# A two-layer row-attention kernel: the first layer's order of work rewritten on every engine, one layer-norm step moved to GpSimd, half the first layer's DVE-copied turns put in a score bank, and an output bias carried into the second layer

## What is computed

```python
x = x + L0(group_norm(x))       # group_norm: 32 groups over all rows, tokens and the group's channels
x = x + L1(group_norm(x))

def L0(x):                      # per row m, 8 heads of 32 channels
    x = layer_norm(x) * norm_w + norm_b                 # over channels
    q, k, v = x @ qkv_w
    weights = softmax(q k + x2d @ x2d_w / sqrt(32))     # 256 x 256 per head, full
    gate = sigmoid(x @ gate_w + gate_b)
    return (weights v * gate) @ final_w + final_b

def L1(x):                      # per row, 4 heads of 64 channels
    q, k, v = x @ w_in + b_in
    weights = softmax(where(|i - j| <= 16, q k / 8, -inf))
    return (weights v) @ w_out + b_out
```

## Time and profile before

| | before |
|---|---|
| median of 3 runs | 3757.91 us (3751.88 to 3758.32) |
| the profiled execution, time | 3752.59 us |
| its span, first to last instruction | 3750.7 us |
| PE busy | 3471.7 us, 93% |
| PEld busy | 3013.3 us, 80% |
| DVE busy | 3122.2 us, 83% |
| ACT busy | 2606.5 us, 69% |
| POOL busy | 1992.7 us, 53% |
| granted TensorE clock, mean | 0.977 |

### The profile page before, as it was taken

How to read it: one execution, slowest core, us unless ns; L and a number is a source line. 1 busy time by engine, 2 the same in 40 slices (tenths; PEclk the granted TensorE clock), 3 DMA queues, 4 the chain that set the end, 5 groups by cost and what they waited for, 6 DMA issues and landing times.

```text
span 3750.7 us, 121088 instructions
## 1 busy us (share of the span) xinstructions
PE 3471.7 (93%) x36234; PEld 3013.3 (80%) x36234; DVE 3122.2 (83%) x11357; ACT 2606.5 (69%) x8615; POOL 1992.7 (53%) x3722
## 2 busy tenths in 40 slices
PE   4469999999999999999999999799999999999998
PEld 1157787787878877787787877699999999999998
DVE  4479999999999999999999999677777777777776
ACT  1158888888888888888888888466666666666665
POOL 0046666676766667666666666333333333333333
PEclk8579999999999999999999999899999999999999
DMA  9911111111111111111111111011111111111111
GB/s 364 359 59 48 50 42 50 42 50 48 44 50 42 50 45 48 50 42 50 42 50 48 44 50 43 29 51 50 50 50 50 50 50 50 50 50 50 50 50 46
DMA packets 189031, 238.40 MB, mean 64 GB/s; under 512 B 11824, under 2 KB 176176, under 8 KB 184752
## 3 DMA queue, kind: packets, MB, share of 16 engines
q1 hardware_dynamic: 184368, 204.17, 17.2%
q10 hardware_dynamic: 4608, 33.56, 2.3%
HBM read 170.57 MB, written 67.11 MB: 63 GB/s over the span
## 4 chain that ended last, share of the span: by engine, by line
PE 50%; DVE 16%; issue 12%; POOL 11%; ACT 5%; DMA 4%; DVEq 1%; ACTq 0%; POOLq 0%; SPq 0%
PE work L458 20%; PE turn L607 7%; POOL prob L354 6%; PE score L590 5%; PE work L467 5%; PE turn L498 5%; PE mix L620 4%; ACT prob L693 4%; PE score L485 3%; DMA x_chunk<-xT 3%; POOL g_tok L368 2%; POOL g_tok L365 2%; DVE kT L936 2%; DVE att L921 2%; DVE y_sb L872 2%
## 5 line engine op out<-in xcount | busy, mean ns | idle before, releaser
L354 POOL TENSOR_SCALAR prob<-prob,row_inv 128x256 f32<-128x256 f32 x2048 | 1049.0, 530 | 682.1 <-DVE row_inv L890 669.6
L458 PE MATMUL work<-src,w 128*128 128x256 f32 x7680 | 1067.5, 288 | 36.9 <-DVE y_sb L872 29.8
L693 ACT ACTIVATE prob<-prob,row_min 128x256 f32<-128x256 f32 x2048 | 1022.8, 504 | 38.9 <-DVE row_min L884 38.8
L458 PEld LDWEIGHTS work<-src,w 128*128 128x128 f32 x7680 | 946.2, 189 | 119.4 <-DVE y_sb L872 59.7
L884 DVE CUSTOM_DVE_ANT_0 prob<-score,neg_bias 128x256 f32<-128x256 f32 x2048 | 753.0, 419 | 111.7 <-PE score L485 100.6
L396 POOL TENSOR_SCALAR prob<-prob,row_inv 128x160 f32<-128x160 f32 x1024 | 387.9, 397 | 814.2 <-DVE row_inv L995 814.2
L756 ACT ACTIVATE prob<-prob,row_min 128x160 f32<-128x160 f32 x1024 | 430.5, 424 | 436.1 <-DVE row_min L988 435.0
L498 PE MATMUL turn<-ident,prob 128*128 128x128 f32 x4096 | 627.3, 276 | 35.3 <-DVE probT L895 29.7
L699 ACT COPY probT<-turn 128x512 f32<-128x512 f32 x512 | 299.4, 585 | 349.8 <-PE turn L498 349.8
L498 PEld LDWEIGHTS turn<-ident,prob 128*128 128x128 f32 x4096 | 463.2, 141 | 78.6 <-POOL prob L354 46.8
L458 PE MATMUL work<-att,wf 128*128 128x256 f32 x3072 | 429.1, 289 | 3.6 <-DVE att L921 2.2
(11 more groups left out here) (86 smaller groups left out, 5021.7 us busy)
## 6 DMA issues: line engine op xcount, KB each, us to landing
pair_chunk<-pairT ACTq DMA_DIRECT2D x32, 1024.0 KB, 7.6
x_chunk<-xT SPq DMA_DIRECT2D x32, 1024.0 KB, 8.0
x_sb<-xT SPq DMA_DIRECT2D x128, 256.0 KB, 3.4
x_tok<-x_nat SPq DMA_DIRECT2D x128, 256.0 KB, 3.4
x1T<-y_sb SPq DMA_DIRECT2D x128, 256.0 KB, 2.2
x_sb<-x1T SPq DMA_DIRECT2D x128, 256.0 KB, 2.9
outT<-y_sb SPq DMA_DIRECT2D x128, 256.0 KB, 2.2
prob<-w_d SPq DMA_DIRECT2D x1, 1024.0 KB, 8.2
```

Source lines behind the costliest of these rows:

```text
L354: pool.tensor_scalar(prob[:, h, ib], prob[:, h, ib], row_inv[:, h, ib:ib + 1], 1.0, ALU.mult, ALU.mult).then_inc(norm_done[0], 1)
L458: ins = pe.matmul(out[:, cb], w[:, of_w, kb, cols + cb * P:cols + (cb + 1) * P], x[:, of_x, kb], start=n == 0, stop=n == len(terms) - 1)
L693: act.activation(prob[:, h, ib], prob[:, h, ib], ACT.Exp, bias=row_min[:, h, ib:ib + 1], scale=-1.0, accum_out=row_sum[:, h, ib:ib + 1]).t ...
```

## The change

All of it but the last item is in the first layer's loop.

- TensorE's order becomes: q(nxt), scores(m, 1), mixes(last, 0), mixes(last, 1), turns(0), t2(far), turns(1), k(nxt), turns(2), turns(3), v(nxt), scores(nxt, 0), turns(4), gate(nxt), turns(5), y(last), turns(6), turns(7). The mixes of a row are thus both done in the turn of the loop after its own.
- turns(3) and turns(7) write the first score bank instead of `turn`. `scores` therefore also waits for DVE's copies of them: scores(m, 1) for the copy of turns(7) of the row before, scores(nxt, 0) for that of turns(3). In return turns(1) and turns(5) directly follow, apart from t2 or the gate, ACT's copy of the turn before them, for which they wait.
- `xn` is computed by GpSimd in place of DVE, in two instructions of 128x256. GpSimd's two steps on `g_tok` work one row further ahead (`ahead`, m+3) and stand apart: the multiplication after norms(m, 1), the addition after norms(m, 2). DVE's layer-norm statistics are for m+3 too, and stand near the end of a turn.
- DVE adds the residual for row m-2 at the start of a turn, as one 128x512 tensor_tensor without a bias in place of two 128x256 instructions with one. The statistics of y are taken every second row, two instructions of 128x512 over two rows, in place of two of 128x256 each row; they stand before the layer-norm statistics, and DVE's last instruction of a turn is the copy of turns(7).
- k uses the same half of `work` as q and the gate; t2, v and y use the other. ACT's order follows.
- The first layer's output bias isn't added to y. The statistics, the second norm's shift and the second layer's output bias (`y_bias`) take it in.

The diff, cut to the order on TensorE, GpSimd and DVE. ACT's reordering, SP's loop and the bias are left out:

```diff
-        gstat1 = sb("gstat1", [P, CB, ROWS, 6])
+        gstat1 = sb("gstat1", [P, CB, ROWS // 2, 6])
...
                 if far.exists:
                     wait(pool, ln_var_done, far.times(1, 1))
                     apart(pool, pool_passed)
                     pool.tensor_tensor(ln_rstd[:], ln_var[:], minus_half[:], ALU.pow).then_inc(ln_rstd_done, 1)
+                    wait(pool, ln_rstd_done, far.times(1, 1))
+                    wait(pool, t2_done, far.times(1, 0))
+                    apart(pool, pool_passed)
+                    for tb in range(TB):
+                        pool.tensor_scalar(xn[:, tb], g_tok[:, far.base % 2, tb], ln_mv[:, tb, 0:1],
+                                           ln_rstd[:, tb:tb + 1], ALU.subtract, ALU.mult).then_inc(xn_done, 1)
+                if m.exists:
+                    norms(m, 1)
+                if ahead.exists:
+
+                    wait(pool, x_tok_in[ahead.base % 2], ahead.times(16, 16, of=2))
+                    wait(pool, xn_done, nxt.times(TB, TB))
+                    apart(pool, pool_passed)
+                    pool.tensor_tensor(g, x_tok[:, ahead.base % 2], gn_row[:, 0].unsqueeze(1).broadcast_to([P, TB, CH]),
+                                       ALU.mult).then_inc(gn_scaled, 1)
+                if m.exists:
+                    norms(m, 2)
+                if ahead.exists:
+                    wait(pool, gn_scaled, ahead.times(1, 1))
+                    pool.tensor_tensor(g, g, gn_row[:, 1].unsqueeze(1).broadcast_to([P, TB, CH]), ALU.add
+                                       ).then_inc(g_done[0], 1)
                 if m.exists:
                     norms(m, 3)
                 if nxt.exists:
                     norms(nxt, 0)
 
-            over_rows(pool, 2, 0, body0)
+            over_rows(pool, 3, 0, body0)
...
+                    wait(pe, turn_done[0][1], r.times(PAIRS0, 2 * hg - 2))
...
                 def turns(h):
                     wait(pe, norm_done[0], m.times(TB * H0, TB * (h + 1)))
-
-                    if h % 2 == 0:
+                    to = turn[:]
+                    if h % HPG == HPG - 1:
+
+                        to = score[:, 0].rearrange("p b t -> p (b t)")
+                        if h < HPG:
+                            wait(pe, min_done[0], m.times(TB * H0, TB * (HPG + 1)))
+                        elif nxt.exists:
+                            wait(pe, min_done[0], nxt.times(TB * H0, TB))
+                    elif h % HPG == 0:
+                        wait(pe, turn_done[0][0], m.times(PAIRS0, h // 2))
+                    elif h % HPG == 1:
+                        wait(pe, turn_done[0][0], m.times(PAIRS0, h // 2 + 1))
+                    else:
                         wait(pe, turn_done[0][1], m.times(PAIRS0, h // 2))
-                    else:
-                        wait(pe, turn_done[0][0], m.times(PAIRS0, h // 2 + 1))
...
+                if nxt.exists:
+                    wait(pe, src_done[0], nxt.times(1, 1))
+                    wait(pe, gate_done, m.times(HG, HG))
+                    project(work[:, 0], w0, 0, x).then_inc(q_ps[0], 1)
                 if m.exists:
                     scores(m, 1)
+                if last.exists:
+                    mixes(last, 0)
+                    mixes(last, 1)
+                if m.exists:
                     turns(0)
-                if last.exists:
-                    mixes(last, 1)
-                if nxt.exists:
-                    wait(pe, src_done[0], nxt.times(1, 1))
-                    project(work[:, 0], w0, 0, x).then_inc(q_ps[0], 1)
+                if far.exists:
+
+                    wait(pe, xn_done, far.times(TB, TB))
+                    wait(pe, y_done[0], m.times(1, -1))
+                    for cb in range(CB):
+                        for tb in range(TB):
+                            ins = pe.transpose(work[:, 1, cb, tb * P:(tb + 1) * P],
+                                               xn[:, tb, cb * P:(cb + 1) * P], ident[:])
+                    ins.then_inc(t2_done, 1)
                 if m.exists:
                     turns(1)
                 if nxt.exists:
-                    wait(pe, gate_done, m.times(HG, HG))
-                    project(work[:, 1], w0, CH, x).then_inc(k_ps[0], 1)
+                    wait(pe, q_done[0], nxt.times(1, 1))
+                    project(work[:, 0], w0, CH, x).then_inc(k_ps[0], 1)
                 if m.exists:
                     turns(2)
-                if nxt.exists:
-                    wait(pe, q_done[0], nxt.times(1, 1))
-                    project_tokens(work[:, 0], w0, 2 * CH, x).then_inc(v_ps[0], 1)
-                if m.exists:
                     turns(3)
                 if nxt.exists:
+                    if far.exists:
+                        wait(pe, xnT_done, far.times(CB, CB))
+                    else:
+                        wait(pe, y_done[0], m.times(1, -1))
+                    project_tokens(work[:, 1], w0, 2 * CH, x).then_inc(v_ps[0], 1)
                     scores(nxt, 0)
                 if m.exists:
                     turns(4)
+                if nxt.exists:
+                    wait(pe, k_done[0], nxt.times(1, 1))
+                    project(work[:, 0], w0, 3 * CH, x).then_inc(gate_ps, 1)
+                if m.exists:
+                    turns(5)
                 if last.exists:
                     wait(pe, att_done[0], last.times(1, 1))
                     if nxt.exists:
-                        wait(pe, k_done[0], nxt.times(1, 1))
-                    elif m.exists:
-                        wait(pe, gate_done, m.times(HG, HG))
+                        wait(pe, v_done[0], nxt.times(1, 1))
                     else:
-                        wait(pe, y_done[0], last.times(CB, 0))
+                        wait(pe, y_done[0], m.times(1, -1))
                     project(work[:, 1], wf0, 0, att).then_inc(y_ps[0], 1)
                 if m.exists:
-                    turns(5)
-                    mixes(m, 0)
-                if far.exists:
-
-                    wait(pe, xn_done, far.times(TB, TB))
-                    wait(pe, v_done[0], nxt.times(1, 1))
-                    for cb in range(CB):
-                        for tb in range(TB):
-                            ins = pe.transpose(work[:, 0, cb, tb * P:(tb + 1) * P],
-                                               xn[:, tb, cb * P:(cb + 1) * P], ident[:])
-                    ins.then_inc(t2_done, 1)
-                if m.exists:
                     turns(6)
-                if nxt.exists:
-                    if last.exists:
-                        wait(pe, y_done[0], last.times(CB, CB))
-                    else:
-                        wait(pe, k_done[0], nxt.times(1, 1))
-                    project(work[:, 1], w0, 3 * CH, x).then_inc(gate_ps, 1)
-                if m.exists:
                     turns(7)
 
             over_rows(pe, 2, 1, body0)
...
+                done = last + -1
+                if done.exists:
+
+                    wait(dve, y_ps[0], done.times(1, 1))
+                    wait(dve, y_out[0][done.base % 2], done.times(16, 0, of=2))
+                    wait(dve, x_in[0][done.base % XSLOTS], done.times(16, 16, of=XSLOTS))
+                    wait(dve, y_stats, done.times(CB, 0, of=2))
+                    apart(dve, dve_passed)
+                    dve.tensor_tensor(y_sb[:, :, done.base % 2], work[:, 1], x_sb[:, done.base % XSLOTS], ALU.add
+                                      ).then_inc(y_done[0], 1)
+                if nxt.exists:
+                    wait(dve, q_high[0], nxt.times(1, 1))
+                    dve.tensor_tensor(nqT[:, nxt.base % 2, LOW], work[:, 0],
+                                      nqT[:, nxt.base % 2, HIGH].bitcast(F32), ALU.subtract).then_inc(q_done[0], 1)
+                if m.exists:
+                    mins(m, 4)
                     inverse(m, 1)
-                    mins(m, 4)
                     mins(m, 5)
+                    mins(m, 6)
+                    mins(m, 7)
...
+                    turn_copy(1, turn[:])
+                if far.exists:
+                    wait(dve, xnT_done, far.times(CB, CB))
+                    wait(dve, gate_ps, far.times(1, -1))
+                    split_high(0, far, xnT[:])
                 if m.exists:
                     inverse(m, 2)
+                if nxt.exists:
+                    wait(dve, k_high[0], nxt.times(1, 1))
+                    dve.tensor_tensor(kT[:, nxt.base % 2, LOW], work[:, 0],
+                                      kT[:, nxt.base % 2, HIGH].bitcast(F32), ALU.subtract).then_inc(k_done[0], 1)
+                if m.exists:
+                    turn_copy(3, score[:, 0].rearrange("p b t -> p (b t)"))
+                if far.exists:
+                    split_low(0, far, xnT[:])
                 if last.exists:
                     wait(dve, att_high[0], last.times(1, 1))
                     dve.tensor_tensor(att[:, LOW], att_sum[:], att[:, HIGH].bitcast(F32), ALU.subtract
```

(33 more changed lines are left out.)

200 lines of the change are left out of this document (78 added, 122 removed).

## The result

| | before | after |
|---|---|---|
| median | 3758.11 us (4 runs, 3751.88 to 3762.64) | 3793.39 us (4 runs, 3789.88 to 3793.92) |
| ratio, 95% interval | | 1.0093 (1.0076 to 1.0111) |
| profiled execution's span | 3750.7 us | 3792.1 us |

The change makes the kernel 0.9% slower. The forecast was 1.9% faster; 3793 lies just inside the range, on the other side. Forms of the same change that ran later (e1, e4 and the runs built on e4, all but f3) are 1.5 to 3.8% faster than before, so the new order is good, and something in the change eats more than it gives.

A forecast was written before the change was run, and what follows sets the result against it. The row was bound by PE's own work plus a chain through DVE's order. 128 x (16.78 - 16.24) = 69 us and 3.5 off 3752.6 gave 3680; medians run 5.3 higher, so 3685 us, range 3615 to 3795.

The forecast's parts named there:

- the price of `xn` on GpSimd: First layer's loop: xn priced like POOL's norms, of the same form and size, at 1.1 us for two instructions.
- the sign that the prediction had named: First layer's loop: t2 waiting for POOL's xn would show the forecast wrong.
- the third rival: xn on POOL too slow: at 1.28 us each a row gets 1.2 longer, 3839 us; chance 0.06.
- a cover of 0.3 us: At t2 and turns(1): t2 can start at 4.4, takes 0.49, and turns(1) isn't due before 5.18.
- PE's row: First layer's loop: PE's new order, added up from start-to-start prices, takes 15.73 us a row.
- The loop through DVE: Copy of turns(7) gates scores(m, 1): loop 15.54 us, 16.74 every second row with y's statistics; mean row 16.24.
- the first rival: PE alone sets the row: both rows 15.73 us, 138 us off, 3620 us; chance 0.13.
- What lies beside: Low parts, residual add, POOL, SP and ACT cost no time; the aggregation behind the loop gets 3.5 us shorter.
- It gives room and no time: xn leaving DVE, 0.73 us for two, comes from a place outside the new loop, so gains no time.
- Held by `g_tok`: POOL's g_tok addition holds DVE's low parts, first mins some 0.9 us late: mean row 17.04, 3787 us; chance 0.20.
- The break-even delay of 0.64: With DVE held by POOL's g_tok step, the kernel is slower than before from a 0.64 us delay per row.
- Most-contended engine: Skill's rule: DVE contended at 92%, PE's weight loads 80%; row falls by xn's 0.73 us on DVE, to 3661 us.

The follow-up runs named there:

- e1: The changed kernel with xn on GpSimd adding the mean instead of subtracting it, so the output differs: 3677.20 us, ratio 0.9787.
- e4: The changed kernel with DVE writing the negated means and GpSimd adding them in xn, same mathematics: 3665.19 us, ratio 0.9751.
- f3: e4 with GpSimd's multiplication on g_tok moved behind norms(m, 2), directly ahead of the addition: 3743.43 us, ratio 0.9967.
- g3: The changed kernel with the subtraction in one of xn's two instructions and an addition in the other: 3707.49 us, ratio 0.9869.
- h1: f1 with g_tok's multiplication behind norms(m, 3) for m+4 and its addition for m+3 directly behind xn: 3614.66 us, ratio 0.9620.
- e2: The changed kernel with xn back on DVE, behind inverse(m, 1), all else kept: 3726.09 us, ratio 0.9919.
- e3: The kernel before with only xn moved to GpSimd, behind the power, with the subtraction and nothing reordered: 3755.67 us, ratio 0.9997.
- f1: e4 with the statistics of y taken each row, two of 128x256, in front of kT's low part: 3657.94 us, ratio 0.9736.
- f2: e4 with the statistics of y taken each row, two of 128x256, at the old place: 3664.38 us, ratio 0.9753.
- g1: f1 with both g_tok steps behind norms(m, 3), for row m+4, and x_tok loaded ahead of storing y: 3665.91 us, ratio 0.9765.
- g2: e4 with both g_tok steps behind norms(m, 3), for row m+4, and x_tok loaded ahead of storing y: 3698.98 us, ratio 0.9847.
- f4: The changed kernel with xn's operations in the other order, multiply then subtract, so the output differs: 3793.73 us (one run).

## Why the prediction was wrong

**The step that failed** is the price of `xn` on GpSimd: "the same form and size with one scalar more: two for 1.1". The form was right and didn't carry the price; the operation did. The rows it rested on are the norms, a multiplication by a multiplication. The trace of before has a still nearer row, in the second layer: a multiplication and an addition with two scalars per partition, in the same size.

```profile
L407 POOL TENSOR_SCALAR g_tok<-x_sb,gn_scale,gn_shift x108: 547/549/552, 3006.9 to 3558.3; 128x256 f32<-128x256 f32 x108
```

That is the forecast's 0.55 to the digit, and it doesn't help either: `xn` took 2.44 for two in place of 1.1. PE then waited for it, the sign that the prediction had named. GpSimd had no subtraction anywhere in the trace of before, so this was an operation that no row showed, and it was to be bounded from the rows of other operations. The 1.28 of a `g_tok` step was such a bound, and it was right beside the measured 1.22. It stood in the text as the third rival, with a chance of 0.06. The chance was the second half of the error: with one bound at 0.5 and one at 1.28 and a cover of 0.3 us, the case deserved far more.

**The rival's mechanism** held. Its formula lets nothing be lost for a while and then the full length; g3 shows a cover of 0.4, against 0.3 in the sum. At 1.28 it gave 3839, and the kernel measured 3793. By the series of g3, 1.28 each instead of 1.22 would be 0.12 a row and 15 us more, 3808. Of the 31 us left, 8 are in the base (e1 has the forecast's own case at 3677, not 3685), and 19 in the larger cover (1.05 lost a row by the series, not 1.2); 4 are not accounted for.

The Trainium skill, in "GPSIMD Engine Reference", section Engine selection, has a one-input step at about line rate and one with two inputs at about twice VectorE's time; it names add, mul and max and gives no price by operation. The runs show 0.55 for multiplication and addition against DVE's 0.41, 1.3 times, and 1.22 for subtraction, 3.0 times; the measurement decides.

**PE's row** was forecast at 15.73 without stalls and is 15.54 to 15.64. Right to 0.01: turns(0) to turns(1), 1.41 for 1.42. Too high: the two mixes, 1.86 for 2.00 (1311.17 to 1313.03 in e4), and turn to turn, 0.44 for 0.49. Too low: turns(1) and turns(4), a turn ahead of a projection, 0.41 for 0.35 (1314.44 to 1314.85 in e4).

**The loop through DVE** was right in kind and nearly in size: 16.48 for 16.74 in the row with the pair, the short row free, mean 16.01 for 16.24. That is 29 us less than forecast over 128 rows. In e4 the ends of the loop take 10 us more than before and the second layer 5 more, to which the prediction had given nothing, so e4's coming within 20 us of 3685 is in part errors that offset each other. The hand-over from the copy of turns(7) to the scores was 0.71 for 0.85 (1326.03 to 1326.74 in e4). h1 shows what the first rival says: with the statistics in a hole of DVE's work, and GpSimd's `g_tok` steps out of its way, both rows are the short one.

**What lies beside.** Removing the bias from the residual add, SP's order and the second bank showed up nowhere as a wait of PE. The aggregation gave its 3.5 us. SP's `x_tok` was to come earlier; with the fast `xn` it comes late: in e4 POOL waits 19.5 us for it in 34 rows, which before it didn't. That wait is POOL's and no time of the row by itself, but it shifts the step on `g_tok` that then meets the cast. "It gives room and no time" for `xn` leaving DVE was wrong in the new order: e2 against e1 says 49 us. A part of that is e2's own meeting of the cast with the `g_tok` step, which was not taken apart from DVE's added work. In the old order it was right (e3).

**Held by `g_tok`** (0.20): true as a mechanism, at three quarters of its price (0.61 a row in f3, 0.8 forecast). The break-even delay of 0.64 leaves out the aggregation's 3.5 us; with them it is 0.67. In after the meeting is with `src`'s cast, 1.52 instead of 0.42 on average, which the rival had put at 0.3 of slack. `kT`'s low part starts at 1317.73, and the scores that need it at 1319.18, so a delay of 1.1 is absorbed there; this is read from the timeline, and no run took that meeting alone away. The Trainium skill, in "GPSIMD Engine Reference", section Specifications, tells of contention with VectorE instructions "in a 2-port perf mode or with two SBUF inputs". The prediction used the second half. The runs agree with the second half: `att` has two SBUF inputs. The cast and the two-element negation have one and are held as well. That they run in such a mode no run shows; the cast's 0.42 beside `att`'s 0.68 for the same 512 elements speaks for it.

**Most-contended engine.** The rule that the prediction cited from "Perfetto Trace Analysis" of the Trainium skill gave 3661, and e4 measured 3665. That agreement isn't evidence for it: in h1 DVE is busy 526 of 560 us and PEld 483, so DVE would be the contended one, yet PE's timeline there is one start after the other with 0.3 us of waiting a row.

**What stays open.** Why the second layer takes 11 us more in after and e1 than before, and 4 to 5 in e4, f3 and h1, with the same instructions. Its waits look alike, and the granted clock is 1.00 from 2500 to 3600 us in before, after, e1, e4 and h1. The runs fall in groups: all seven with the additional small tile `ln_neg` (e4, f1, f2, f3, g1, g2, h1) are at 1325, and after, e1, f4, g3 and e2 without it, in the same new order, at 1331 to 1332. So neither the length of `xn` nor the place of the statistics sets it, and what the tile or its instruction moves was not tried. In one row around 3000 us, k's twelve matmuls take 1.61 from start to start in after and 1.54 before, v's 1.51 and 1.47, with no wait shown at either. Of the 41.4 us between the spans 13 lie behind the aggregation, so about a third of the difference isn't the `xn` wait. Without that wait (e1) the same second layer is in a kernel 2.1% faster, so the verdict doesn't hang on it.

## What to carry to other kernels

Price a moved instruction by its operation on the engine that it goes to; where the trace has no row of that operation there, take the far bound for likely, and look how much cover it has. If a subtraction must go to GpSimd, write the negated value on the engine that has it and add. Put GpSimd's two-tensor steps beside DVE work that reads PSUM, one at a time, and check every small DVE instruction in their way.

## What the runs showed of the hardware

- GpSimd, `tensor_scalar` of 128x256 f32 with two per-partition scalars: addition and multiplication 0.55 us (before's second layer, e1, e4), a subtraction in either position 1.22 (after, f4).
- While GpSimd does a `tensor_tensor` of 128x512 (1.28 us), a DVE instruction that reads SBUF through a cast, through two tensors, or as a `tensor_scalar` of two elements ends only after it: 0.42 to 1.52, 0.68 to 1.77, 0.17 to 0.91. DVE's reads of PSUM beside it keep their length (`mins` 0.42 in h1). So do two instructions that read SBUF alone: the layer-norm statistics (0.75 for two, at 1309.59 in g1) and the reciprocals (0.17, at 1321.10 in after).
- It goes the other way for GpSimd's `tensor_scalar`. In the same row of after, four norms take 2.90 instead of 1.85 where DVE's two low parts (1318.91 to 1320.19, both from SBUF) run, and those keep their 0.68. In e4 the first of the two takes 0.82 there and the second 0.68.
- The scores of the same second layer spanned 1319 to 1320 us (before, e3), 1325 (the seven runs with `ln_neg`) or 1331 to 1332 (after, e1, e2, f4, g3), by the kernel around it.
